# Reordering the first batch's chain of a two-layer mixture-of-experts kernel, with TensorE kept at work before it

## The chip, the cores and the metric

The kernel runs on one core of a Trainium2 chip. The metric is device microseconds for the whole program, the median of three runs.

## The reference

Eight sequences of 1024 tokens with 256 channels, in fp32, go through a "macaron" block: a feed-forward layer, an attention layer, and the same feed-forward layer again with the same weights.

```
x = x + 0.5 * ffn(layernorm(x))
x = x + attention(layernorm(x))       # 16 heads, relu(q), relu(k), linear attention
x = x + 0.5 * ffn(layernorm(x))
ffn(x):
  scores = softmax(x @ gate_w.T);  s = scores + gate_b      # 16 experts in 4 groups
  keep the 2 best groups (sum of their 2 best s), of those the 2 best experts
  y = sum over the 2 experts: scores[e] * ((silu(x@We1[e]+be1[e]) * (x@We3[e]+be3[e])) @ We2[e] + be2[e])
  z = (silu(x@ws1+bs1) * (x@ws3+bs3)) @ ws2 + bs2           # shared expert, 256 inner channels
  return y + z
```

## The kernel before, in words

Names in the text: PE is TensorE, DVE VectorE, ACT ScalarE, POOL GpSimd, SP SyncE (it only issues DMAs). A batch is one of the eight sequences; it has NT = 8 tiles of 128 tokens, and a half is four of them. `r` counts batches over both layers (0 to 15), `L` is the layer, `b` the batch in it.

The program is written by hand engine by engine. Every engine has its own list of instructions, and semaphores (`wait_ge`, `then_inc`) tie them together. One feed-forward layer has two stages: `route(L)` and `experts(L)`.

`route` normalises each batch (DVE takes statistics, POOL raises them to the power -0.5 as `rstd`, DVE makes `nmr`, ACT writes the normalised rows), PE transposes it in four groups `transpose(r, n)` of four 128x128 tiles into the bank `xT_ps`, and ACT copies each group to the transposed activations (`copy_xT`). `gate(r)` on PE makes the scores, DVE copies them (L1188), PE turns them (`turn_scores`), and DVE's generator `choices` picks the experts in some 30 small operations, with one `Exp` on ACT in between. It ends in `sel`; PE's `rank(r)` counts places from it; DVE's `slots(r)` makes the row numbers; ACT's `meta` writes three extra columns; and POOL's `scatter` sends the batch's rows to their expert's region in DRAM, in 16 indirect DMAs, two halves of 8. With `let_through` POOL stops after four sends of each half, and before a batch, until PE has come to a certain part.

Beside all this runs the shared expert, cut in six parts a batch: `up` parts (PE L540, eight instructions of 512 columns each; ACT's silu L896; DVE's gated product L1311) and `down` parts (PE L556, DVE adds to x, L1321). The table `FIRST` says which parts stand in which batch's turn. For later batches DVE takes the choices in small steps between the parts. For batch 0 it does all choices and only then the first two gated products, and PE, which may run only one `up` part ahead of them, does the transposes of batch 1 in one go and waits.

A buffer of normalised rows serves every third batch (`XS` = 3): `normalise(r)` on ACT first waits until the scatter of batch r - 3 has landed. The choices for batch r include the statistics of batch r + 2.

Set-up: POOL writes the constants (identity, ones, and so on) and signals `setup_done`. ACT's queue loads batch 0 in two halves and then the small weights. SP's queue loads `half_bs2` and all biases; with the first half of x landed it issues batch 1, then waits for the biases' split in three bf16 parts by DVE (`bias_split`), stores them, issues batch 2, waits for the store, loads `bias_rows`, and issues the other batches, the experts' weights and the padding. DVE splits the biases first, then does the two halves' statistics of batch 0 (`half_stats`), the first `nmr`, the carry, the second `nmr`, and the statistics of batch 1. The split's scratch memory is in `m.xn`, which is also batch 0's transposed activations, so ACT's first copy waits until the parts are stored.

Of the kernel before, what the change touches and what calls it, by code (L numbers as in the profile page):

```python
# [20 lines left out]
P = 128  # L21
# [285 lines left out]
def program(nc, m, d, sem):  # L307
# [52 lines left out]
    bias_f, bias_r = m.xn[:, 0, 0:nb], m.xn[:, 1, 0:nb]  # L360
    bias_p = m.xn[:, 2, :].bitcast(BF16)[:, 0:3 * nb].rearrange("p (k n) -> p k n", k=3)
# [13 lines left out]
    def piece(n):  # L375
        b, h = divmod(n, PIECES)
        return x_tiles(b, h * NT // PIECES, NT // PIECES)

# [12 lines left out]
    with nc.Block() as block:  # L391
        @block.sync
        def _(sp):
# [54 lines left out]
            sp.wait_ge(s.setup_done, 1)  # L448
# [41 lines left out]
        def _(pe):  # L490
            def transpose(r, n):
                g, c = divmod(n, KC)
                pe.wait_ge(s.xn_half, 2 * r + g + 1)
                wait(pe, s.xT_copied, 4 * r + n)
                if n == 0:
                    wait(pe, s.rank_read, r - 1)
                    if early(r):
                        pe.wait_ge(s.a_xT_copied, 4 * (2 * (r - BATCHES) + 2))
                    if r == BATCHES + EARLY:
                        pe.wait_ge(s.a_xT_copied, 4 * BATCHES)  # L500
                for j in range(4):
                    last = nc.tensor.transpose(xT_ps[:, j * P:(j + 1) * P],
                                               m.xs[buffer_of(r)][:, 4 * g + j, c * P:(c + 1) * P], m.ident[:])
                last.then_inc(s.xT_ready, 1)
# [97 lines left out]
            def route(L):  # L602
                for b in range(LEAD[L], BATCHES):
# [20 lines left out]
                    if b == LEAD[L]:  # L624
                        if L:
                            shared(L, n, turn_and_first_half)
                            shared(L, n + 1, second_half)
                        else:
                            gate(r)
                            shared(L, n, turn)  # L630
                            shared(L, n + 1)
                            for j in range(4):
                                transpose(r + 1, j)
                        rank(r)
                        for j in range(n + 2, end):
                            shared(L, j)
                        continue
# [155 lines left out]
            for n in range(4):  # L793
                transpose(0, n)
# [64 lines left out]
        def _(act):  # L859
# [15 lines left out]
            def copy_xT(r, n):  # L875
# [4 lines left out]
                elif r == 0:  # L880
                    act.wait_ge(s.bias_bounced, 16)
# [6 lines left out]
                nc.scalar.copy(m.xnTs[xnT_of(r)][:, c, g * HALF:(g + 1) * HALF], xT_ps[:]).then_inc(s.xT_copied, 1)  # L888
# [21 lines left out]
            def route(L):  # L910
                for b in range(LEAD[L], BATCHES):
                    r = L * BATCHES + b
                    more = b + 1 < BATCHES
                    n, end = FIRST[L][b - LEAD[L]:b - LEAD[L] + 2]
                    if more:
                        normalise(r + 1)
                    if b == LEAD[L]:
                        exponentials(r)
                        if L:
                            copy_xT(r + 1, 0)  # L920
                        shared(L, n)
                        if L:
                            copy_xT(r + 1, 1)
                            copy_xT(r + 1, 2)
                        shared(L, n + 1)
                        for j in range(3 if L else 0, 4):
                            copy_xT(r + 1, j)
# [180 lines left out]
        def _(dve):  # L1108
# [81 lines left out]
            def route_work(r):  # L1190
# [6 lines left out]
                if ahead:  # L1197
                    yield from stats_work(r + 2)
                yield from choices(r)
# [137 lines left out]
            def route(L):  # L1337
                for b in range(LEAD[L], BATCHES):
# [3 lines left out]
                    if b == LEAD[L]:  # L1342
# [3 lines left out]
                        shared(L, n + 1, iter(()), 0)  # L1346
                        for _ in slots(r):
# [121 lines left out]
            dve.wait_ge(s.bias_loaded, 16)  # L1469
            nc.vector.tensor_copy(bias_p[:, 0], bias_f).then_inc(s.bias_split, 1)  # L1470
            dve.wait_ge(s.bias_split, 1)
            ch.then(TT(bias_r, bias_f, bias_p[:, 0], ALU.subtract))
            nc.vector.tensor_copy(bias_p[:, 1], bias_r).then_inc(s.bias_split, 1)
            dve.wait_ge(s.bias_split, 2)
            ch.then(TT(bias_f, bias_r, bias_p[:, 1], ALU.subtract))
            nc.vector.tensor_copy(bias_p[:, 2], bias_f).then_inc(s.bias_split, 1)
            ch.did(nc.vector.memset(m.ones_b[:], 1.0))
            ch.then(nc.vector.memset(m.sel[:], 0.0))
            def half_stats(h, arrived, ready):
                tiles = slice(h * PAIRS, (h + 1) * PAIRS)  # L1480
                dve.wait_ge(arrived, 16)
                stats(0, range(h * PAIRS, (h + 1) * PAIRS))
# [12 lines left out]

            half_stats(0, s.x_first, s.first_stats)
            half_stats(1, s.x_in[0], s.stats_ready)
# [336 lines left out]
```

## Time and profile before

| | us |
|---|---|
| median of three runs | 1282.25 (1281.26 to 1282.93) |
| the profiled execution, its own time | 1280.93 |
| its span, first to last instruction | 1279.2 |
| PE busy | 1148.5 |
| DVE busy | 860.4 |
| ACT busy | 762.1 |
| POOL busy | 696.8 |

Busy times are of the span; several engines work at once. The mean granted clock of TensorE is 0.973 of full speed. The chain of waits is the list of work that ended last, followed back from the end: only time on it can be saved. A timeline lists an engine's instructions with start and duration, and merges equal ones.

### The profile page before, as it was taken

The page shows a single profiled execution, that of the slowest core. Times are in us where ns is not written, and L with a number is a line of the kernel's source. Part 1 is how long each engine was busy: PE and PEld are TensorE (multiplying, and loading weights), DVE is VectorE, ACT ScalarE, POOL GpSimd, SP SyncE. Part 2 cuts the span into 40 slices and gives each one's busy share as a digit, 9 for nine tenths or more (in the row PEclk, how much of TensorE's full clock was granted, in tenths as well). Part 3 has the DMA queues.
Part 4 walks back from the last instruction along what each step waited for, and adds up shares of the span by engine and source line. Part 5 has one row for each costly group of instructions (what it writes and reads, how often), then busy time and mean ns, then how long its engine had stood idle before and what let it go on. Part 6 is the DMA issues. An engine that isn't in the chain of part 4 may idle for free.

```text
span 1279.2 us, 26244 instructions
## 1 busy us (share of the span) xinstructions
PE 1148.5 (90%) x6640; PEld 899.7 (70%) x6640; DVE 860.4 (67%) x2772; ACT 762.1 (60%) x1700; POOL 696.8 (54%) x850
## 2 busy tenths in 40 slices
PE   4897989899999994999998999899799999999981
PEld 2554555699999974777887878555456999999750
DVE  4686777366666645677778776676753766666487
ACT  4344542388888846575665653544313888888488
POOL 3366767388888873010421503256661888887820
PEclk9899989999999997999999999999999999999996
DMA  9822225656655533011311400012277566555398
GB/s 347 281 76 88 96 84 145 190 174 175 171 172 164 160 96 120 32 67 66 104 64 34 129 21 34 34 67 80 88 204 259 167 172 172 170 166 154 100 400 354
DMA packets 93928, 181.53 MB, mean 142 GB/s; under 512 B 17592, under 2 KB 60368, under 8 KB 91990
## 3 DMA queue, kind: packets, MB, share of 16 engines
q1 hardware_dynamic: 66342, 110.44, 28.2%
q0 software_dynamic: 26016, 67.55, 15.2%
q10 hardware_dynamic: 1424, 1.86, 0.5%
q8 instruction: 59, 0.97, 0.3%
q14 instruction: 87, 0.71, 0.2%
HBM read 97.63 MB, written 86.08 MB: 144 GB/s over the span
## 4 chain that ended last, share of the span: by engine, by line
PE 58%; DVE 17%; ACT 10%; POOL 6%; issue 5%; DMA 3%; SPq 1%; DVEq 0%; ACTq 0%; POOLq 0%
PE bank L681 20%; PE bank L691 10%; PE bank L540 7%; POOL expert_rows L1623 5%; PE bank L556 5%; PE bank L672 5%; PE bank L787 3%; ACT rows L979 2%; PE bank L737 2%; ACT w L979 2%; DVE stat L1120 2%; PE bank L713 2%; ACT xn L997 1%; ACT rows L870 1%; PE bank L515 1%
## 5 line engine op out<-in xcount | busy, mean ns | idle before, releaser
L1686 POOL DMA_INDIRECT routed_rows<-xn,rdest x286 | 282.6, 988 | 114.7 <-DVE xn L1414 44.5
L681 PE MATMUL bank<-rows,att 128*128 128x128 f32 x2288 | 302.4, 275 | 0.4 <-ACT att L968 0.4
L681 PEld LDWEIGHTS bank<-rows,att 128*128 128x128 f32 x2288 | 278.3, 192 | 1.1 <-ACT att L968 0.9
L1623 POOL DMA_INDIRECT expert_rows<-rows,slots x160 | 154.8, 967 | 105.7 <-issue 56.1
L968 ACT COPY att<-w 128x512 f32 x286 | 177.1, 619 | 12.2 <-issue 6.4
L691 PE MATMUL bank<-w,rows 128*128 x572 | 170.8, 381 | 1.6 <-DVE rows L1401 1.4
L1401 DVE SCALAR_TENSOR_TENSOR rows<-bank,tile_b,att 128x128 f32<-128x128 f32 x286 | 100.1, 350 | 107.2 <-ACT att L973 96.4
L967 ACT COPY rows<-bank 128x256 f32<-128x256 f32 x286 | 106.4, 372 | 83.3 <-PE bank L672 77.6
L1414 DVE TENSOR_TENSOR xn<-bank,be 128x256 f32<-128x256 f32 x286 | 121.5, 425 | 33.8 <-issue 11.1
L556 PE MATMUL bank<-ws,be 128*128 128x256 f32 x512 | 124.7, 394 | 8.5 <-DVE be L1311 8.4
L556 PEld LDWEIGHTS bank<-ws,be 128*128 128x128 f32 x512 | 98.6, 197 | 39.5 <-DVE be L1311 17.8
L896 ACT ACTIVATE silu<-bank,bs 128x512 f32<-128x512 f32 x64 | 43.9, 686 | 133.7 <-PE bank L540 133.5
L1675 POOL TENSOR_TENSOR xres<-xres,half_bs 128x128 f32<-128x128 f32 x256 | 117.9, 469 | 3.0
L672 PE MATMUL bank<-ident,rows 128*128 128x128 f32 x572 | 109.0, 273 | 3.1 <-DVE xres L1321 2.1
L973 ACT ACTIVATE att<-bank,tile_b 128x128 f32<-128x128 f32 x286 | 103.5, 362 | 3.8 <-PE bank L681 3.8
L672 PEld LDWEIGHTS bank<-ident,rows 128*128 128x128 f32 x572 | 80.0, 141 | 32.0 <-issue 3.5
L691 PEld LDWEIGHTS bank<-w,rows 128*128 128x128 f32 x572 | 87.0, 192 | 2.6 <-issue 2.5
L1311 DVE SCALAR_TENSOR_TENSOR be<-bank,bs,silu 128x512 f32<-128x512 f32 x64 | 47.8, 750 | 59.1 <-PE bank L540 57.6
L1623 POOL DMA_INDIRECT expert_rows<-w,slots x48 | 48.2, 1004 | 60.3 <-PE bank L713 29.8
L979 ACT ACTIVATE rows<-rows,weights 128x256 f32<-128x256 f32 x176 | 73.7, 498 | 10.2 <-DMA rows<-routed_rows 10.2
L540 PE MATMUL bank<-w,ws 128*128 128x512 f32 x160 | 76.1, 607 | 1.2 <-DVE be L1311 1.2
L1611 POOL TENSOR_TENSOR rstd<-ve,minus_half 128x8 f32<-128x8 f32 x8 | 15.0, 1878 | 113.7 <-DVE ve L1128 113.7
(206 smaller groups left out, 2028.9 us busy)
## 6 DMA issues: line engine op xcount, KB each, us to landing
rows<-expert_rows SPq DMA_DIRECT2D x286, 129.5 KB
rows<-routed_rows SPq DMA_DIRECT2D x32, 512.0 KB, 4.0
w<-routed_rows SPq DMA_DIRECT2D x10, 1024.0 KB, 9.8
w<-in_w SPq DMA_DIRECT2D x2, 4096.0 KB, 18.1
out<-xres SPq DMA_DIRECT2D x16, 512.0 KB, 9.1
xres<-in_x SPq DMA_DIRECT2D x7, 1024.0 KB, 7.2
rows<-routed_rows SPq DMA_DIRECT2D x6, 1024.0 KB, 7.3
expert_rows<-pad SPq DMA_DIRECT2D x47, 129.5 KB, 5.9
```

The source lines that it names most:

```text
L540: last = nc.tensor.matmul(bank[:], ws[:, c, mi * P:(mi + 1) * P], xnT[:, c, g * HALF:(g + 1) * HALF], start=c == 0, stop=c == KC - 1)
L556: last = nc.tensor.matmul(y_ps[j][:, t % 2 * C:(t % 2 + 1) * C], m.gT[:, g, mi, t * P:(t + 1) * P], m.ws2[:, mi, :], start=mi == 0, stop=m ...
L672: last = nc.tensor.transpose(rT_ps[a % 2][:, c * P:(c + 1) * P], m.rin[:, a % SLOTS, c * P:(c + 1) * P], m.ident[:])
L681: last = nc.tensor.matmul(rh_ps[t % RB][:, n * P:(n + 1) * P], m.rw13[:, t % RB, c * C + n * INTER:c * C + (n + 1) * INTER], m.rT[:, t % R ...
L691: nc.tensor.matmul(ry_ps[y % RB][:, 0:C], m.rgT[:, y % RB, :], m.w2[:, bass.ds(e, C)], start=True, stop=True).then_inc(s.ry_ready, 1)
L967: nc.scalar.copy(m.rT[:, a % RB, :], rT_ps[a % 2][:, 0:C]).then_inc(s.rT_copied, 1)
L968: nc.scalar.copy(m.rw13[:, a % RB, :].rearrange("p (c n) -> p c n", c=KC), w13[:, :, bass.ds(expert_at(i + 2), C)]).then_inc(s.rw13_copied, 1)
L979: last = nc.scalar.activation(y[:, k, j * C:(j + 1) * C], y[:, k, j * C:(j + 1) * C], ACT.Copy, scale=m.weights[:, b, k, i:i + 1])
L1414: TT(m.ry[:, n, :], ry_ps[y % RB][:, 0:C], m.be2[:, bass.ds(e, C)], ALU.add).then_inc(s.ry_scaled, 1)
L1623: nc.gpsimd.indirect_dma_start(out=d.xg, out_offset=bass.IndirectOffsetOnAxis(ap=m.slots[:, slots_of(r), k, i:i + 1], axis=0), in_=m.xs[bu ...
L1675: last = nc.gpsimd.tensor_tensor(x, x, m.half_bs2[:, c:c + P], ALU.add)
L1686: nc.gpsimd.indirect_dma_start(out=d.yt, out_offset=bass.IndirectOffsetOnAxis(ap=m.rdest[:, n:n + 1], axis=0), in_=m.ry[:, n, :], in_offse ...
```

## The change

Four things change, all in the first layer's first batch.

1. The biases' scratch moves to `m.att`, and ACT's first copy no longer waits for the store. DVE splits the biases after batch 0's statistics. SP issues batch 1 at the set-up's end, batch 2 when the first half of x has landed, and the small `bias_rows` load after the experts' weights.
2. In batch 0 the transposes go in turn to two banks (`xT_of`); DVE copies groups 0 and 1, ACT groups 2 and 3. ACT normalises the second half before any copy. DVE makes the first `nmr` before it aggregates the second half.
3. In batch 0's turn PE does batch 1's transposes inside parts 2 and 3 and the rank behind part 3. DVE does the choices in steps, six before each of the first two gated products, and a part of batch 2's statistics ahead of the first step. ACT normalises half of batch 1, then does the exponentials, the first silu, the other half.
4. `keep_busy` puts products of constants on PE, with results nobody reads: 20 before the first transposes, 4 after groups 0 and 1, 4 after groups 2 and 3.

```diff
-    bias_f, bias_r = m.xn[:, 0, 0:nb], m.xn[:, 1, 0:nb]
+    scratch = m.att[:, NT * ROW:NT * ROW + 4 * nb]
+    bias_f, bias_r = scratch[:, 0:nb], scratch[:, nb:2 * nb]
...
+    def xT_of(r, n):
+        return y_ps[0] if r == 0 and n % 2 else xT_ps
...
+            sp.wait_ge(s.setup_done, 1)
+            load_x(1)
             sp.wait_ge(s.x_first, 16)
-            load_x(1)
+            load_x(2)
             sp.wait_ge(s.bias_split, 3)
             sp.dma_start(d.bias_parts.rearrange("k (p f) -> p k f", p=P), bias_p).then_inc(s.bias_bounced, 16)
-            load_x(2)
-            sp.wait_ge(s.bias_bounced, 16)
-            sp.wait_ge(s.rows_zeroed, 1)
-            sp.dma_start(m.bias_rows[0:3, :], d.bias_parts[:, BPROJ:BPROJ + C]).then_inc(s.bias_placed, 16)
...
-                wait(pe, s.xT_copied, 4 * r + n)
+                wait(pe, s.xT_copied, 4 * r + n if r else n // 2 * 2)
...
                             shared(L, n + 1)
-                            for j in range(4):
-                                transpose(r + 1, j)
+                            shared(L, n + 2, first_half)
+                            shared(L, n + 3, second_half)
                         rank(r)
-                        for j in range(n + 2, end):
+                        for j in range(n + (2 if L else 4), end):
                             shared(L, j)
...
             pe.wait_ge(s.setup_done, 1)
-            for n in range(4):
-                transpose(0, n)
+            def keep_busy(count):
+                for _ in range(count):
+                    nc.tensor.matmul(h3_ps[1][:, 0:P], m.ones_f[:], m.ident[:], start=True, stop=True)
+            keep_busy(20)
+            transpose(0, 0)
+            transpose(0, 1)
+            keep_busy(4)
+            transpose(0, 2)
+            transpose(0, 3)
+            keep_busy(4)
...
-                elif r == 0:
-                    act.wait_ge(s.bias_bounced, 16)
...
+                    if r == 0:
+                        normalise(1, range(PAIRS))
+                        exponentials(0)
+                        shared(0, n)
+                        normalise(1, range(PAIRS, NT))
+                        shared(0, n + 1)
+                        copy_xT(1, 0)
+                        shared(0, n + 2)
+                        for j in range(1, 4):
+                            copy_xT(1, j)
+                        meta(0)
+                        for j in range(n + 3, end):
+                            shared(0, j)
+                        continue
...
-            copy_xT(0, 0)
             normalise(0, range(PAIRS, NT))
-            for n in range(1, 4):
+            for n in range(2, 4):
                 copy_xT(0, n)
...
+                chosen, ahead_stats = choices(r), stats_work(r + 2) if ahead else iter(())
+                if r == 0:
+                    next(ahead_stats)
+                    next(ahead_stats)
+                    next(chosen)
+                    yield
+                    next(ahead_stats)
+                    for _ in range(5):
+                        next(chosen)
+                        yield
...
-                    if b == LEAD[L]:
+                    if r == 0:
+                        shared(0, n, work, 6)
+                        shared(0, n + 1, work, 6)
+                        for _ in work:
+                            pass
+                    elif b == LEAD[L]:
...
+            dve.wait_ge(s.x_first, 16)
+            stats(0, range(PAIRS))
+            half_aggregate(0, s.first_stats)
+            dve.wait_ge(s.x_in[0], 16)
+            stats(0, range(PAIRS, NT))
             half_negate_mean(0, s.first_rstd, s.first_nmr)
+            half_aggregate(1, s.stats_ready)
+            split_bias()
             dve.wait_ge(s.setup_done, 1)
             ch.then(nc.vector.tensor_copy(m.carry[:], m.region0[:]))
             half_negate_mean(1, s.rstd_ready, s.nmr_ready)
+            for n in range(2):
+                dve.wait_ge(s.xT_ready, n + 1)
+                nc.vector.tensor_copy(m.xnTs[0][:, n, 0:HALF], xT_of(0, n)[:]).then_inc(s.xT_copied, 1)
             route_stats(1)
```

## Rows read from the trace of the kernel before

**Rows 1.** The page, part 4: the chain's share of the span by engine.
```profile
PE 58%; DVE 17%; ACT 10%; POOL 6%; issue 5%; DMA 3%; SPq 1%; DVEq 0%; ACTq 0%; POOLq 0%
```

**Rows 2.** Chain of waits, 70 to 330 us: start, duration, what.
```profile
77.72 0.95 POOL expert_rows L1623
...
98.39 2.45 DMA expert_rows<-rows,slots
```

**Rows 3.** POOL's timeline, 40 to 250 us: start, duration, instruction, idle and releaser.
```profile
43.53 1.21 POOL L1623 DMA_INDIRECT expert_rows<-rows,slots  x1 [11.95 <-issue]
...
58.85 1.67 POOL L1605 TENSOR_TENSOR rstd<-ve,minus_half 128x8 f32<-128x8 f32 x1 [5.26 <-DVE ve L1128]
...
125.74 0.95 POOL L1623 DMA_INDIRECT expert_rows<-rows,slots  x1 [4.39 <-DVE slots L1172]
...
175.47 0.96 POOL L1623 DMA_INDIRECT expert_rows<-att,slots  x1 [5.79 <-DVE slots L1172]
```

**Rows 4.** Chain of waits, 40 to 60 us.
```profile
40.47 6.28 PE bank L540 x8
...
50.21 3.43 PE bank L540 x8
53.64 1.00 PE bank L515 x16
```

**Rows 5.** Timeline of all engines, 0 to 75 us.
```profile
6.82 0.33 SPq L397 DMA_DIRECT2D xres<-in_x  x1
...
8.63 1.41 DVE L1120 BATCH_NORM_STATS2 stat<-xres 128x6 f32<-128x256 f32 x4
...
10.74 1.04 POOL L1736 TENSOR_TENSOR rstd<-ve,minus_half 128x4 f32<-128x4 f32 x1 [6.20 <-DVE ve L1487]
...
12.49 0.15 DVE L1492 SCALAR_TENSOR_TENSOR nmr<-mv,rstd 128x4 f32<-128x4 f32 x1
```

**Rows 6.** Line 1031, batch 0's two loads: from issue to landing.
```profile
DMA to landing us min/median/max: 6.0/6.7/7.5
```

**Rows 7.** Windows, PE: window, length, busy (count), granted clock, DMA share, GB/s.
```profile
39.00:40.00 1.00, 0.58 (x8) 0.50 1.07 459
...
46.00:47.00 1.00, 1.00 (x4) 1.00 0.90 307
```

**Rows 8.** DVE's timeline, 20 to 60 us.
```profile
24.98 0.42 DVE L1188 COPY tile_b<-bank 128x256 f32<-128x256 f32 x1 [4.41 <-PE bank L515]
...
28.92 0.29 DVE L1206 TENSOR_REDUCE mx<-bank 128x8 f32<-128x128 f32 x1
...
35.92 0.29 DVE L1154 TENSOR_TENSOR chosen<-rev,rr 128x128 f32<-128x128 f32 x1
...
39.58 1.41 DVE L1311 SCALAR_TENSOR_TENSOR be<-bank,bs,silu 128x512 f32<-128x512 f32 x2
...
48.52 0.69 DVE L1321 SCALAR_TENSOR_TENSOR xres<-bank,xres 128x512 f32<-128x512 f32 x1 [0.92 <-PE bank L556]
```

**Rows 9.** PE's timeline, 60 to 260 us.
```profile
62.64 0.60 PE L502 MATMUL bank<-ident,att 128*128 128x128 f32 x4
...
75.53 0.44 PE L523 MATMUL bank<-ident,tile_b 128*128 128x128 f32 x2 [1.52 <-DVE tile_b L1188]
...
117.48 0.30 PE L577 MATMUL bank<-sel,before 128*128 128x144 bf16 x1 [3.59 <-DVE sel L1250]
...
118.19 1.94 PE L515 MATMUL bank<-xnT,gate_w 128*32 128x256 f32 x16
...
221.22 1.05 PE L588 MATMUL bank<-ident,tabf 128*128 128x128 f32 x8
```

**Rows 10.** Timelines of ACT and DVE, 50 to 130 us.
```profile
72.51 4.04 ACT L870 ACTIVATE rows<-xres,nmr,rstd 128x256 f32<-128x256 f32 x8 [1.65 <-DMA expert_rows<-rows,slots]
...
81.18 0.31 ACT L901 ACTIVATE ex<-sh 128x128 f32<-128x128 f32 x1 [3.33 <-DVE sh L1207]
...
96.88 0.17 DVE L1172 CAST slots<-slot_f 128x16 uint32<-128x16 f32 x1
```

More of the change, by code:

```diff
@@ L447, in _ @@
                          .to_broadcast([P, E * C // 2])).then_inc(s.be2_in, 16)
-            sp.wait_ge(s.setup_done, 1)
+            sp.wait_ge(s.bias_bounced, 16)
+            sp.wait_ge(s.rows_zeroed, 1)
+            sp.dma_start(m.bias_rows[0:3, :], d.bias_parts[:, BPROJ:BPROJ + C]).then_inc(s.bias_placed, 16)
             for i in range(SPARE_TILES):
@@ L501, in transpose @@
                 for j in range(4):
-                    last = nc.tensor.transpose(xT_ps[:, j * P:(j + 1) * P],
+                    last = nc.tensor.transpose(xT_of(r, n)[:, j * P:(j + 1) * P],
                                                m.xs[buffer_of(r)][:, 4 * g + j, c * P:(c + 1) * P], m.ident[:])
@@ L887, in copy_xT @@
                     act.wait_ge(s.ay_ready, BATCHES * PAIRS)
-                nc.scalar.copy(m.xnTs[xnT_of(r)][:, c, g * HALF:(g + 1) * HALF], xT_ps[:]).then_inc(s.xT_copied, 1)
+                nc.scalar.copy(m.xnTs[xnT_of(r)][:, c, g * HALF:(g + 1) * HALF], xT_of(r, n)[:]).then_inc(s.xT_copied, 1)
             def shared(L, n):
@@ L918, in route @@
                         exponentials(r)
-                        if L:
-                            copy_xT(r + 1, 0)
+                        copy_xT(r + 1, 0)
                         shared(L, n)
-                        if L:
-                            copy_xT(r + 1, 1)
-                            copy_xT(r + 1, 2)
+                        copy_xT(r + 1, 1)
+                        copy_xT(r + 1, 2)
                         shared(L, n + 1)
-                        for j in range(3 if L else 0, 4):
-                            copy_xT(r + 1, j)
+                        copy_xT(r + 1, 3)
                         meta(r)
@@ L1196, in route_work @@
                 yield from placing
-                if ahead:
-                    yield from stats_work(r + 2)
-                yield from choices(r)
+                chosen, ahead_stats = choices(r), stats_work(r + 2) if ahead else iter(())
[8 more added lines that the diff above has]
+                        yield
+                yield from ahead_stats
+                yield from chosen
                 if ahead:
@@ L1468, in _, with half_aggregate @@
             nc.vector.memset(m.bias_rows[:, :].bitcast(U32), 0).then_inc(s.rows_zeroed, 1)
[L1469 to L1476, printed above, removed]
             ch.did(nc.vector.memset(m.ones_b[:], 1.0))
             ch.then(nc.vector.memset(m.sel[:], 0.0))
-            def half_stats(h, arrived, ready):
+            def half_aggregate(h, ready):
                 tiles = slice(h * PAIRS, (h + 1) * PAIRS)
-                dve.wait_ge(arrived, 16)
-                stats(0, range(h * PAIRS, (h + 1) * PAIRS))
                 ch.settle()
@@ L1494, in half_negate_mean, with split_bias @@
                 dve.wait_ge(ready, 1)
-            half_stats(0, s.x_first, s.first_stats)
-            half_stats(1, s.x_in[0], s.stats_ready)
+            def split_bias():
+                dve.wait_ge(s.bias_loaded, 16)
+                nc.vector.tensor_copy(bias_p[:, 0], bias_f).then_inc(s.bias_split, 1)
+                dve.wait_ge(s.bias_split, 1)
+                ch.then(TT(bias_r, bias_f, bias_p[:, 0], ALU.subtract))
+                nc.vector.tensor_copy(bias_p[:, 1], bias_r).then_inc(s.bias_split, 1)
+                dve.wait_ge(s.bias_split, 2)
+                ch.then(TT(bias_f, bias_r, bias_p[:, 1], ALU.subtract))
+                nc.vector.tensor_copy(bias_p[:, 2], bias_f).then_inc(s.bias_split, 1)
+            dve.wait_ge(s.x_first, 16)
[3 more added lines that the diff above has]
+            stats(0, range(PAIRS, NT))
             half_negate_mean(0, s.first_rstd, s.first_nmr)
+            half_aggregate(1, s.stats_ready)
+            split_bias()
             dve.wait_ge(s.setup_done, 1)
```

3 lines of the change are left out of this document (2 added, 1 removed).

## The prediction

> **What bounds the kernel now.** I read the page's shares first, then the chain of waits, then the timelines of each engine over the first 100 us. By the page PE leads the chain for 58% [rows 1]: a saving beside PE's path is lost unless it moves PE, or whatever paces PE. The chain [rows 2] tells which: up to about 74 us it runs through the set-up, DVE's choices for batch 0 and PE; from 77.72 us through POOL's scatters of routed rows. Those pace the rest of the first routing. Scatter(1)'s last send, 98.39, has landed at 100.84, then ACT normalises batch 4 into the same buffer, then come batch 3's choices and scatter(3) at 125.74, scatter(5) at 175.47, and from there sends without a gap to the last of this routing [rows 3]. Each is released by the one before, so whatever moves 77.72 moves the experts' start and, behind it, the end. Sends are 1.265 us apart and not shortened by the change.
>
> So two numbers decide: when gate(1), batch 1's first product on PE, starts (53.64 us now, [rows 4]), since part 9, whose first half releases scatter(1), follows it after 24.1 us (77.72 - 53.64) of PE work at full rate; and whether POOL is free by then.
>
> **Front: to batch 0's scores.** Now SP sees the first half of x at 6.82, but DVE splits the biases until 8.5 and starts statistics at 8.63; its nmr comes at 12.49 [rows 5]. After the change statistics start at about 6.9. From their start to POOL's power took 10.74 - 8.63 = 2.11, so POOL works from 9.0 to 10.05. DVE now does the second half's statistics (1.40) before nmr, and these need the second half of x. The two halves, issued at 0.8 and 1.25, took 6.0 to 7.5 us to land [rows 6]: 6.8 and about 8.7. The load of batch 1 (1 MB) is issued at set-up's end, 4.6 instead of 6.82, so its data meet this half. Bounds: no delay (statistics 9.0 to 10.4), or the 1.9 us between the landings doubled, 10.6 (to 12.0). I take 9.5, nearer the undisturbed landing: nmr from 10.9 to 11.05, 1.4 us earlier than now. The layer's weights follow x on ACT's queue; 1 MB at the 459 GB/s of [rows 7] makes them 2.3 later at most. No group of waits names them now, and gate(0) is covered by DVE (below), so I count nothing.
>
> The second half, alone among large loads, landed 1.9 us behind the first [rows 6], 512 KB in that time. The Trainium skill (DMA: Bandwidth & Descriptors, Queues, rings and completion order) says that a DMA engine takes turns between the queues that hold work for it, packet by packet. By that rule, which speaks against moving batch 1's load forward, the sum would be 1.1 us worse than with my 9.5; without it 0.5 us better.
>
> Then DVE: aggregate and ve to 11.7, POOL's power 11.8 to 12.8, meanwhile the five split operations (bounded by SP's 6.82 and the statistics' 8.63 in [rows 5], two memsets included; I take 1.1) and the carry to 12.95, second nmr 13.1. ACT normalises 11.1 to 13.2 and 13.25 to 15.3 (2.07 each). Transposes 0 and 1 go to two banks without waiting for a copy. DVE copies them: no row has a DVE copy of 128x512. Bounds are ACT's 0.58 and twice the 0.42 of DVE's 128x256 copy; I take 0.69, the time of DVE's 128x512 add out of the same memory [rows 8]. So 13.95 to 15.35. Transposes 2 and 3 follow ACT's second half at 15.4, gate(0) comes at about 17.3 instead of 22.90. But that is not what counts: DVE must finish batch 1's statistics before it copies the scores: 3.59 from the first to after ve (the same work stands between the copy's end at 25.33 and 28.92, [rows 8]), 1.67 for POOL's power [rows 3], and 0.5 for two handovers and nmr. 15.35 + 5.75 = 21.1 against 24.98 now. **Gain 3.9 us.** PE waits for this inside its first part.
>
> **Batch 0's choices.** Now, from the copy of the scores to gate(1), 53.64 - 24.98 = 28.66 us. DVE does all choices, then the first two gated products at 39.58; PE's third part waits for them, and runs at half clock: granted clock 0.50 from 39 on, 1.00 only from 46, after a stretch (34 to 38.7) of four short groups of transposes between copies; eight products take 6.28 us where eight take 3.43 later [rows 4, 7]. After: DVE's work until the second gated product has ended is copy 0.35, statistics of batch 2 3.59 (25.33 to 28.92), choices up to the first rr 7.0 (28.92 to 35.92), two gated products of 0.70 (1.41 for both, [rows 8]): 12.35, at 33.45. The steps are cut so that six come before each of the two. Exp is no wait of its own: ACT normalises only four tiles of batch 1 (2.07) before it, and its silu with the table load (1.3 + 0.7) ends two us before the first gated product. The other PE operations up to here are covered: 1.72 to the turn, 5.2 behind it, 4.33 for part 2 with two transposes, with some 2 us of idle in all. Then PE at full rate: part 3 with two groups of transposes 3.45 + 0.88, rank 0.5, part 4 3.45 (each from [rows 4, 9]): gate(1) is 12.35 + 0.05 + 4.33 + 0.55 + 3.45 = 20.75 after the copy of the scores. **Gain 28.66 - 20.75 = 7.9 us.** From 35.92 to the first gated product at 39.58 were 3.66, with sel, the weights and nmr: sel is done before 33.45 + 3.66 = 37.1, rank comes at 37.85: no wait.
>
> Together gate(1) at 21.1 + 20.75 = 41.85, **11.8 us earlier**.
>
> **Products of constants.** No row has this one; the nearest is L588, 128x128 with ident, eight instructions in 1.05 us, and four products of 128 columns are eight instructions [rows 9]: 0.22 us a product at full rate, 0.44 at half. Twenty from 4.6: 4.4 to 8.8 us, over at 9.0 to 13.4; first transposes come at 13.2. Cost 0 to 0.2, hidden by the front's DVE and ACT. The fours cost 0.9 (1.8 cold), after transposes 1 and 3: the first lies beside ACT's second half, the second beside ACT's two copies; cold, gate(0) is delayed by about 1.0, within DVE's cover (PE idle 1.4 before the turn). If clock is not raised by them, gate(0), 1.0 at full rate, costs 1.97 and the first half part 3.4: 22.7, the logits 0.3 late: cost 0 to 0.5. I take 0. Their value is mostly insurance: the order already removes the sparse stretch. PE is idle some 1.5 us at three places; behind 1.52 idle the rate stayed full, behind 3.59 not (L515's group took 1.94, against 1.00 in [rows 4]) [rows 9].
>
> **SP and POOL.** x(2) goes to 6.9, the bias parts and x(3) onward to 13, at most 1.4 earlier than now; the placing of the biases moves behind the expert loads, needed only in the attention. SP's new early wait for the set-up holds back only loads that now go at 6.82 or later; the pads still follow everything. POOL: slots(0) 1.55 after rank, 40.0; first send 1.1 later at 41.1. Now from 43.53 sixteen sends of 1.265 with rstd in between (1.67 and 0.3) take 22.2, without the wait of 5.26 before 58.85 (for batch 3's statistics, which then are there at 46): POOL free at 63.3. Scatter(1) is wanted at 77.72 - 11.8 = 65.9: 2.6 us of cover. The place of `bias_f` in other memory takes a wait off ACT's first copy; its price lies between 0 and 1.3 (the copy came 12.49 + 3.5), and the front above doesn't use it.
>
> What is late next: normalise(3) needs scatter(0) landed, 2.8 after its last send at 62.3: 65.1, against 72.51 - 11.8 = 60.7 [rows 10]. It ends with its table load at 70.5; exp(2) could start at 81.18 - 11.8 = 69.4. DVE's choices 1.1 late; slots(2) end at 97.05 and the send that needs them is at 99.66 (98.39 + 1.27) [rows 2, 10], so 2.6 hides 1.1.
>
> **Sum.** 3.9 + 7.9 = 11.8 us off the profiled execution's 1280.93 (span 1279.2, 1.7 around it): 1269.1. The median of the runs, 1282.25, lies 1.3 higher; from it 1270.4, which I predict for the changed kernel's median.
>
> **Rivals.**
> - *The scatter loop keeps part* (0.13): normalise(3) comes only 7.4 us earlier. If its lateness of 4.4 is passed on by ACT's order (copies and silu behind exp) past the 2.6 of cover, the gain is 7.4 to 10: 1274.9. For: ACT waits for landed sends in each batch from here. Against: the slack at slots(2), and normalise(4), which depends on scatter(1), not on scatter(0).
> - *The front gives nothing* (0.09): the load of x late, or DVE copying and splitting ahead of batch 1's statistics eats the gain; only 7.9 stays: 1274.4. Against: two copies are 1.4 us and the split 1.1, both counted.
> - *Better than I count* (0.08): load undisturbed (0.5), DVE's copies at 0.58 (0.2), and a later latency of PE or DVE shortened where the loop's two gaps on POOL (4.4 at 125.74, 5.8 at 175.47) shrink with the new phase, by 1.5 of their 10.2: 1268.2.
> - *Slower: the clock* (0.04): PE's many short idles keep it at half from gate(0) on. Content from there to gate(1) is 1.0 + 0.22 + 4 x 3.45 + 3.45 + 1.76 + 0.5 = 20.8 at full rate, 41.5 at half: gate(1) at 17.3 + 41.5 = 58.8, 5.2 late: 1287.5. It turns slower when more than 13.8 of the 20.8 run at half (11.8 gained and 2 of idle). For: a sparse stretch did this at 39. Against: busy share after 17.3 is about 0.9.
> - *It does nothing* (0.03): scatter pace set elsewhere, another wait at 77.72: 1282.
>
> **Chances.** Forecast 0.63 (its own range 1268.5 to 1272.5, by the bounds of the load, -0.5 to +1.1, and of the copies, -0.2 to +0.3). Range 1266.5 to 1277: it holds the best counting and the two partial cases, and leaves out the clock and no effect; 8 in 10 or a bit more, as the DMA and copy bounds make it. What this kernel's measurement can tell from no change is 0.2%, 2.6 us: faster 0.92, within 0.04, slower 0.04.
>
> **What would show it.** nmr at 10.9; scores copied at 21.1; rate of L540 at 0.43 a product from gate(0); second gated product at 33.4; gate(1) at 41.9; first send 41.1; scatter(1) at 65.9; scatter(3) at 113.9, scatter(5) at 163.7; experts the same in length. Wrong if gate(1) moves and 77.72 moves less, or if the later scatters don't follow.

## The result

| | before | after |
|---|---|---|
| median of the runs, us | 1282.05 (4 runs, 1281.26 to 1282.93) | 1268.8 (4 runs, 1268.31 to 1271.33) |
| profiled execution, its own time and span | 1280.93, 1279.2 | 1268.79, 1267.1 |

The ratio is 0.9895, with a 95% interval from 0.9882 to 0.9907: 13.3 us faster by the medians, 12.1 by the profiled executions. Predicted were 1270.4 and a gain of 11.8. The single marks stand as follows.

| mark, start in us | before | forecast | after | moved by |
|---|---|---|---|---|
| first nmr | 12.49 | 10.9 | 10.10 | -2.4 |
| batch 0's scores copied | 24.98 | 21.1 | 20.03 | -5.0 |
| gate(1) | 53.57 | 41.9 | 40.23 | -13.3 |
| first send | 43.53 | 41.1 | 39.52 | -4.0 |
| scatter(1) | 77.72 | 65.9 | 64.55 | -13.2 |
| scatter(3) | 125.74 | 113.9 | 113.90 | -11.8 |
| scatter(5) | 175.47 | 163.7 | 162.38 | -13.1 |
| last send of the first routing | 235.04 | | 221.94 | -13.1 |
| first send of the experts' results | 254.10 | | 241.51 | -12.6 |

The page of the changed kernel has the same shape as before [rows 1].

```profile
span 1267.1 us, 26351 instructions
...
PE 56%; DVE 18%; ACT 9%; POOL 6%; issue 5%; DMA 4%; SPq 1%; DVEq 0%; ACTq 0%; POOLq 0%
```

The timeline of all engines, 0 to 75 us, shows the new front; it answers to [rows 5] and [rows 8]. Read DVE from its statistics at 6.85 to the second gated product at 30.97.

```profile
4.62 2.48 SPq L401 DMA_DIRECT2D xres<-in_x  x2
4.64 6.08 PE L799 MATMUL bank<-ident,ones_f 128*128 128x128 f32 x40 [4.64 <-POOLq L1775]
...
6.85 1.40 DVE L1141 BATCH_NORM_STATS2 stat<-xres 128x6 f32<-128x256 f32 x4 [5.57 <-DMA xres<-in_x]
...
8.78 1.40 DVE L1141 BATCH_NORM_STATS2 stat<-xres 128x6 f32<-128x256 f32 x4
...
10.10 0.14 DVE L1519 SCALAR_TENSOR_TENSOR nmr<-mv,rstd 128x4 f32<-128x4 f32 x1
...
12.40 1.09 PE L506 MATMUL bank<-ident,rows 128*128 128x128 f32 x8 [1.68 <-ACT rows L1059]
13.16 1.29 DVE L1546 COPY xn<-bank 128x512 f32<-128x512 f32 x2 [0.93 <-PE bank L506]
...
14.37 2.70 DVE L1141 BATCH_NORM_STATS2 stat<-xres 128x6 f32<-128x256 f32 x8
...
16.73 1.07 PE L519 MATMUL bank<-xn,gate_w 128*32 128x256 f32 x16 [0.18 <-DMA bs<-in_bs]
...
18.16 1.64 POOL L1650 TENSOR_TENSOR rstd<-ve,minus_half 128x8 f32<-128x8 f32 x1 [6.18 <-DVE ve L1149]
...
20.03 0.42 DVE L1209 COPY tile_b<-bank 128x256 f32<-128x256 f32 x1
...
30.97 0.75 DVE L1341 SCALAR_TENSOR_TENSOR be<-bank,bs,silu 128x512 f32<-128x512 f32 x1
...
31.77 1.13 PE L560 MATMUL bank<-ws,be 128*128 128x256 f32 x4 [0.47 <-DVE be L1341]
```

The second half's statistics at 8.78 carry no idle time: batch 1's early load, issued at 4.62, did not hold them up. Gate(0) at 16.73 runs at full rate (1.07 for sixteen), 3.3 us before DVE can copy its scores.

From 38 to 260 us the chain of waits is what paces the rest; it answers to [rows 2] and [rows 4]. The half clock of 39 to 46 us is gone, but two later places keep theirs (L519 is the gate, L560 the down part).

```profile
60.40 2.63 DMA expert_rows<-rows,slots
63.12 4.04 ACT rows L883 x8
...
85.19 2.79 DMA expert_rows<-rows,slots
...
105.50 1.87 PE bank L519 x16
107.37 3.21 PE bank L560 x8
...
154.67 1.86 PE bank L519 x16
156.54 2.52 PE bank L560 x8
```

The same chain before, 118 to 174 us, has 2.30 us for the down part (L556 there) behind batch 3's gate and 3.73 for that behind batch 5's:

```profile
120.13 2.30 PE bank L556 x8
...
168.43 3.73 PE bank L556 x8
```

So scatter(3) lost 0.9 us to the clock and scatter(5) got 1.2 back. That is most of the difference between the moves: -13.2 at scatter(1), -11.8 at scatter(3), -13.1 at scatter(5). That scatter(3) stands on its forecast to the hundredth is luck: it was 1.3 us ahead at scatter(1) and lost them on the way. POOL's timeline, 30 to 250 us, shows its idle time before scatter(1), 3.19 us where 2.6 were forecast [rows 3].

```profile
39.52 1.21 POOL L1668 DMA_INDIRECT expert_rows<-rows,slots  x1 [8.59 <-issue]
...
49.60 1.68 POOL L1650 TENSOR_TENSOR rstd<-ve,minus_half 128x8 f32<-128x8 f32 x1
...
64.55 0.96 POOL L1668 DMA_INDIRECT expert_rows<-rows,slots  x1 [3.19 <-PE bank L560]
...
113.90 0.96 POOL L1668 DMA_INDIRECT expert_rows<-rows,slots  x1 [5.84 <-DVE slots L1193]
...
162.38 0.96 POOL L1668 DMA_INDIRECT expert_rows<-att,slots  x1 [4.72 <-DVE slots L1193]
```

### The profile page after: what moved, and what is told of

It is laid out like the page before. It is cut to its first block, busy times and chain, and to the rows that moved or that the text cites. A ratio compares the mean times of both kernels' runs of the same rounds, so it can differ in the third digit from the quotient of the medians.

```text
span 1267.1 us, 26351 instructions
## 1 busy us (share of the span) xinstructions
PE 1149.6 (91%) x6696; PEld 904.2 (71%) x6696; DVE 862.2 (68%) x2774; ACT 761.6 (60%) x1698; POOL 696.6 (55%) x850
## 4 chain that ended last, share of the span: by engine, by line
PE 56%; DVE 18%; ACT 9%; POOL 6%; issue 5%; DMA 4%; SPq 1%; DVEq 0%; ACTq 0%; POOLq 0%
PE bank L685 20%; PE bank L695 10%; PE bank L544 5%; PE bank L560 5%; PE bank L676 5%; POOL expert_rows L1668 5%; PE bank L791 3%; PE bank L741 2%; ACT rows L1001 2%; DVE stat L1141 2%; PE bank L717 2%; ACT rows L883 1%; ACT xn L1019 1%; DMA expert_rows<-rows,slots 1%; DMA w<-routed_rows 1%
## 5 line engine op out<-in xcount | busy, mean ns | idle before, releaser
L1450 DVE TENSOR_TENSOR xn<-bank,be 128x256 f32<-128x256 f32 x286 | 121.5, 425 | 35.0 <-issue 13.1
L560 PE MATMUL bank<-ws,be 128*128 128x256 f32 x512 | 124.9, 394 | 8.5 <-DVE be L1341 8.5
L560 PEld LDWEIGHTS bank<-ws,be 128*128 128x128 f32 x512 | 98.4, 197 | 40.0 <-DVE be L1341 18.6
## 6 DMA issues: line engine op xcount, KB each, us to landing
w<-routed_rows SPq DMA_DIRECT2D x10, 1024.0 KB, 12.1
```

The costliest lines, as they stand in the source:

```text
L560: last = nc.tensor.matmul(y_ps[j][:, t % 2 * C:(t % 2 + 1) * C], m.gT[:, g, mi, t * P:(t + 1) * P], m.ws2[:, mi, :], start=mi == 0, stop=m ...
L1450: TT(m.ry[:, n, :], ry_ps[y % RB][:, 0:C], m.be2[:, bass.ds(e, C)], ALU.add).then_inc(s.ry_scaled, 1)
```

## The experiments

Whole times scatter by several us from run to run on the chips used here (the kernel before: 1276.6 to 1288.3), while gate(1) and the last send of the first routing agree within 0.3 us in the two profiles of the changed kernel (e0 below). So each experiment is read by its ratio and, for its place, by these two marks. They have noise of their own: e4 has the front of the kernel before, unedited, and yet its first nmr is at 13.07 instead of 12.49. In between, single transfers vary more. Batch 0's last send takes 2.63 us to land in the changed kernel's profile and 5.44 in e8's, ahead of anything e8 adds. Each experiment has one profile, so differences under about 0.6 us at a mark are not told from nothing.

| run | ratio to before (95%) | gate(1) | last send |
|---|---|---|---|
| before | 1 | 53.57 | 235.04 |
| changed | 0.9895 (0.9882 to 0.9907) | 40.23 | 221.94 |
| e0 changed, again | 0.9901 (0.9884 to 0.9917) | 40.27 | 222.22 |
| e1 no products | 0.9919 (0.9897 to 0.9940) | 42.33 | 223.21 |
| e2 products alone | 1.0015 (1.0001 to 1.0029) | 51.73 | 233.38 |
| e3 old order of the choices | 0.9956 (0.9929 to 0.9984) | 48.25 | 230.41 |
| e4 new order alone | 0.9945 (0.9926 to 0.9965) | 47.94 | 229.57 |
| e11 front alone | 0.9962 (0.9949 to 0.9976) | 48.38 | 230.11 |
| e5 batch 1's load later | 0.9897 (0.9869 to 0.9925) | 40.37 | 222.44 |
| e6 split first | 0.9919 (0.9892 to 0.9946) | 41.41 | 223.38 |
| e7 one bank | 0.9912 (0.9884 to 0.9941) | 41.24 | 223.61 |
| e10 twenty products only | 0.9906 (0.9888 to 0.9924) | 40.46 | 221.10 |
| e8 products before two ranks | 0.9878 (0.9851 to 0.9904) | 40.15 | 221.45 |
| e9 products at four idles | 0.9874 (0.9855 to 0.9893) | 40.38 | 218.86 |

**The parts, taken out or put in alone.** e1 takes the products out of the changed kernel:

```diff
-            keep_busy(20)
             transpose(0, 0)
             transpose(0, 1)
-            keep_busy(4)
             transpose(0, 2)
             transpose(0, 3)
-            keep_busy(4)
```

> The changed kernel without the 28 products of constants. My theory (order and front carry the gain, the products almost nothing): gate(0) starts at 16.7 as now but at half clock, so the gate and the first half part take 2.0 + 3.4 us, the logits come at 22.5 instead of 20.95 and DVE, ready at 21.7, waits 0.8 us; part 3 starts some 0.6 later. 0.6 to 1.4 us slower than the changed kernel, 1269.6. Rival (the clock carries the gain): the granted clock stays at half through batch 0's parts and 5 us or more are lost, 1274 or above.

Gate(1) came 2.1 us later: more than forecast, far less than the rival's 5. Its PE timeline, 10 to 40 us:

```profile
12.64 1.94 PE L506 MATMUL bank<-ident,rows 128*128 128x128 f32 x8 [12.64 <-ACT rows L1056]
15.46 1.94 PE L506 MATMUL bank<-ident,rows 128*128 128x128 f32 x8 [0.88 <-DVE xn L1543]
18.17 1.93 PE L519 MATMUL bank<-xn,gate_w 128*32 128x256 f32 x16 [0.77 <-ACT xn L896]
20.03 3.47 PE L544 MATMUL bank<-xn,ws 128*128 128x512 f32 x4
23.34 0.38 PE L527 MATMUL bank<-ident,tile_b 128*128 128x128 f32 x2
```

I had counted the gate and the half part, and left out the transposes: each group of eight takes 1.94 instead of about 1.07, so gate(0) is at 18.17 and the turn (L527) at 23.34 instead of 20.51. The loss comes in two pieces. DVE's copies of the transposes end 0.9 us later, and with them its statistics of batch 1 and the copy of the scores (20.89 instead of 20.03). Then DVE waits 1.13 us for the turn. At the last send 1.3 of the 2.1 us are left, because rank, gate and down part of batch 3 took 0.7 us less in e1: there the gate ran at full rate (1.00). e2 puts the same products into the kernel before:

```diff
-            for n in range(4):
-                transpose(0, n)
+            keep_busy(20)
+            transpose(0, 0)
+            transpose(0, 1)
+            keep_busy(4)
+            transpose(0, 2)
+            transpose(0, 3)
+            keep_busy(4)
```

> The kernel before with only the 28 products of constants, put at the same places of PE's order. My theory: transposes and gate of batch 0 run at the full rate, the copy of the scores moves from 24.98 to about 22.5, the chain behind it keeps its length and its half clock at 39 to 46; 2.0 to 2.8 us faster than before, 1279.7. Rival (the clock carries the gain): PE stays at full clock from there on and 5 us or more are gained, 1277 or below. Second rival: nothing, because the front hangs on ACT and DVE.

Gate(1) moved by 1.84 and the last send by 1.66, a little under the forecast; the total didn't get faster. Between the last send and the end its profile is 3.7 us longer than that of before, and e0 (below) shows that this stretch varies by such an amount in one and the same kernel. But twelve runs against 22 put the ratio at 1.0001 to 1.0029, which leaves out the forecast gain of 2 us. The 1.7 us of the last send did not reach the end, and why stays open. Its windows of PE (length, busy and count, granted clock, DMA share, GB/s) show that they did not hold the clock among the old order's single transposes:

```profile
14.00:16.00 2.00, 0.66 (x4) 1.00 0.75 230
16.00:18.00 2.00, 1.74 (x10) 0.68 0.97 385
18.00:20.00 2.00, 1.73 (x8) 0.50 0.98 406
20.00:22.00 2.00, 1.45 (x12) 0.97 1.04 430
```

e3 is the changed kernel with batch 0's turn as before, e4 the kernel before with only that turn new, both on all three engines. Of e3's edit, PE's part is shown; ACT's and DVE's orders go back in the same way:

```diff
...
                             shared(L, n + 1)
-                            shared(L, n + 2, first_half)
-                            shared(L, n + 3, second_half)
+                            for j in range(4):
+                                transpose(r + 1, j)
                         rank(r)
-                        for j in range(n + (2 if L else 4), end):
+                        for j in range(n + 2, end):
...
```

> The changed kernel with batch 0's turn as before (all choices first, batch 1's transposes in one go, rank before part 2), front and products kept. My theory: the copy of the scores stays at 20.0, the chain from it to gate(1) takes 28.7 instead of 20.2 us again, with the sparse stretch and half clock in it: 8.4 us slower than the changed kernel, 1277.2. Rival (the scatter loop sets the pace, and part of the order's gain is lost in it anyway): 5 to 7 us slower, 1275.

> The kernel before with only batch 0's turn in the new order; old front, no products. My theory: the copy of the scores at 24.98 as before, gate(1) 20.2 to 21 us after it instead of 28.7: 7.7 to 8.4 us faster than before, 1274. Rival (without products PE is cold for the parts and the order gains little): 3 to 5 us faster, 1278.

e3: gate(1) 8.0 later, close to the forecast of 8.4. The last send is 8.5 later and the total some 0.6% slower: little is lost in the scatter loop. e4: 5.6 earlier, where 7.7 to 8.4 were forecast and 3 to 5 by the rival; gate(1) follows the copy of the scores (25.56) after 22.4 instead of 20.2 us. PE was at half rate at the start of batch 0, and in the new order that costs: the turn comes 3.35 us behind the copy, 0.48 in the changed kernel. Another 0.6 is the late front named above, so the order itself gave 6.2 (28.6 - 22.4). e11 is the third part alone, the changed kernel with the edits of e1 and e3 together:

> The kernel before with only the new front (split later, loads earlier, two banks with DVE's two copies): old order of batch 0's turn, no products. If parts add up: products alone gave gate(1) 1.84 earlier and the order alone 5.6 of the 13.34, so the front has up to 5.9; with the products it gave 5.3. Without them I expect gate(1) 3.2 to 4.2 us earlier than before (49.4 to 50.4). Rival (the front hangs on DVE alone): 5.3 earlier also without products.

It gave 5.2, the rival's value, not mine: with the old order the products add only 0.1 to the front at gate(1) (48.38 against 48.25). They do bring the third part 0.7 us forward (35.35 in e3, 36.08 in e11), but this part then takes 5.9 us in e3 and 5.3 in e11, because e3's half clock set in earlier. PE's windows, e3 first, then e11:

```profile
30.00:32.00 2.00, 1.14 (x5) 0.50 1.10 475
```

```profile
30.00:32.00 2.00, 1.08 (x8) 1.00 0.99 426
```

In e11 the granted clock stands at 0.50 only from 34 us. That both effects nearly cancel is an outcome of these two profiles, not a rule. At gate(1) the parts alone give 1.8 + 5.6 + 5.2 = 12.6 of 13.3, so they nearly add, though which of them is paid for the clock depends on the company it is in. In the totals they add less well: by the ratios e2 has +0.15%, e4 -0.55% and e11 -0.38%, together -0.8% where the whole change has -1.05%.

**Inside the front.** e5 delays batch 1's load, e6 moves the split ahead, e7 goes back to one bank:

```diff
             sp.wait_ge(s.setup_done, 1)
+            sp.wait_ge(s.x_first, 16)
             load_x(1)
-            sp.wait_ge(s.x_first, 16)
             load_x(2)
```

```diff
+            split_bias()
             dve.wait_ge(s.x_first, 16)
...
             half_aggregate(1, s.stats_ready)
-            split_bias()
```

```diff
-                wait(pe, s.xT_copied, 4 * r + n if r else n // 2 * 2)
+                wait(pe, s.xT_copied, 4 * r + n)
...
-        return y_ps[0] if r == 0 and n % 2 else xT_ps
+        return xT_ps
```

> The changed kernel with batch 1's load issued only when the first half of x has landed (6.85 instead of 4.62 us). In the changed kernel's trace the second half's statistics start at 8.78 with no wait, so the early load did not delay them: no difference (-0.3 to +0.3). Rival (large loads share the queues' turns): the second half and the weights, whose last one gate(0) waited 0.18 for, land sooner, and 0.3 to 0.6 us are gained. Second rival: batch 1's statistics at 14.37 then wait for its landing, up to 2 us lost.

> The changed kernel with the biases' split ahead of batch 0's statistics, as before. The first nmr moves from 10.10 to about 11.5 (statistics start at 8.3 instead of 6.85), and everything up to gate(1) with it, since the later place of the split (10.77 to 11.85) lay beside POOL's power: 1.4 us slower. Rival: the split's 1.1 us were on DVE's path either way, and DVE had 0.93 us of idle before its copies: 0 to 0.5 us slower.

> The changed kernel with batch 0's transposes in one bank again, each waiting for the copy before it; DVE still copies groups 0 and 1, ACT 2 and 3. The second transposes start when DVE's first copy ends (13.82) instead of at once, so DVE's second copy and batch 1's statistics behind it come 0.7 to 0.9 later, and everything to gate(1) with them: gate(1) at 41.0, 0.8 slower. Rival: DVE's time is set by POOL's power for batch 1, and ACT's two copies in turn delay gate(0) only: no difference.

e5: no difference at gate(1) (0.14 later, ratio 0.9897), first theory right. The loads themselves do differ. Of the layer's weights, which follow x on ACT's queue, the slowest load landed 10.9 us after its issue in the changed kernel and 6.1 in e5 (7.9 in the kernel before). This is the line of these loads (L1056), first in the changed kernel, then in e5:

```profile
DMA to landing us min/median/max: 5.6/8.3/10.9
```

```profile
DMA to landing us min/median/max: 4.9/5.2/6.1
```

So batch 1's early load holds the weights up by about 4.8 us. Gate(0) waits for them 0.18 us in the changed kernel, 0.88 in e3 and 1.33 in e10, and it costs nothing only because DVE copies the scores later still. e6: 1.2 later at gate(1), as at the first nmr (11.27): the theory was off by 0.2, the rival wrong. e7: 1.0 later at gate(1) and at the copy of the scores (21.03), of which 0.1 was there at the first nmr, so the second bank is worth about 0.9. The wait for POOL's power is 1.88 us in both profiles. It moves with DVE's statistics ahead of it and doesn't hide the delay.

e10 leaves only the first twenty products.

```diff
             transpose(0, 1)
-            keep_busy(4)
             transpose(0, 2)
             transpose(0, 3)
-            keep_busy(4)
```

> The changed kernel with the first 20 products and without the two groups of four. If the first twenty raise the clock and the transposes after them hold it, gate(0) comes 0.0 to 0.3 earlier and nothing else moves: gate(1) at 40.0 to 40.2. Rival (the fours are needed to hold the clock over the idle beside ACT and DVE): the gate or a part falls to half rate, and gate(1) comes 1 to 2 us later.

Gate(1) 40.46 against 40.23, of which 0.21 was there at the first nmr, and the gate at full rate (1.07 in the PE timeline of 4 to 24 us, below). The fours are not needed here. Gate(0) came no earlier, as I had expected, but 0.5 us later (17.21), because it waited 1.33 for the last weight.

```profile
4.64 7.11 PE L799 MATMUL bank<-ident,ones_f 128*128 128x128 f32 x40 [4.64 <-POOLq L1773]
12.62 1.09 PE L506 MATMUL bank<-ident,rows 128*128 128x128 f32 x8 [0.86 <-ACT rows L1057]
14.82 1.06 PE L506 MATMUL bank<-ident,rows 128*128 128x128 f32 x8 [1.11 <-DVE xn L1544]
17.21 1.07 PE L519 MATMUL bank<-xn,gate_w 128*32 128x256 f32 x16 [1.33 <-DMA bs<-in_bs]
```

**Where the clock still falls.** e8 and e9 put products into the idle time of PE that the chain shows before ranks 3 and 5 (e9 also before layer 2's rank 13, and 68 before the attention's first transposes):

```diff
             def rank(r):
                 ranks = ranks_of(r)
-                pe.wait_ge(s.sel_ready, r + 1)
                 if not early(r):
                     pe.wait_ge(s.xT_copied, 4 * (r + 1 if r % BATCHES == BATCHES - 1 else r + 2))
+                if r in (3, 5):
+                    for _ in range(14):
+                        nc.tensor.matmul(xT_ps[:, 0:P], m.ones_f[:], m.ident[:], start=True, stop=True)
+                pe.wait_ge(s.sel_ready, r + 1)
```

```diff
             pe.wait_ge(s.bias_placed, 16)
+            pe.wait_ge(s.rT_copied, TILES)
+            for _ in range(68):
+                nc.tensor.matmul(xT_ps[:, 0:P], m.ones_f[:], m.ident[:], start=True, stop=True)
             for n in range(4):
                 a_transpose(0, n)
```

> The changed kernel with 14 more products of constants (3.0 us at full rate) before the ranks of batches 3 and 5, where PE is idle for 3.6 us waiting for sel and then runs the rank, the gate and part of a down part at half clock (gate 1.87 instead of 1.00, eight products of L560 3.21 and 2.52 instead of 1.73). My theory: the chain of waits runs through just these, so 2.3 us at batch 3 and 1.7 at batch 5 come back and pass through the scatter loop to the end: 2.5 to 4 us faster than the changed kernel, 1265.5. Rival: POOL's unbroken sends or the experts' loads set the end of the routing, and less than 1 us is gained.

> The changed kernel with products of constants at every long idle of PE: 15 before the ranks of batches 3 and 5 and of batch 5 of layer 2, and 68 (14.6 us at full rate) in the 16.7 us in which PE waits for the attention's first transposes. In e8 the two of layer 1 moved scatter(5) by 2.9 us but the last send by 0.5 only, and the total by about 2. My theory: the attention's start, two groups of four transposes at 0.97 and twelve products at 3.11 us on the chain, gives 2 to 2.5 us more, layer 2's rank 1 to 2: 4 to 6 us faster than the changed kernel, 1264. Rival: what comes behind (ACT's weighing, POOL's sends, DVE's choices) takes it back, as in e8, and it is level with e8, 1267.

e8's products worked locally. In its PE timeline, 96 to 116 us, gate and down part are at full rate (3.37 us of products instead of idle):

```profile
102.15 3.37 PE L582 MATMUL bank<-ident,ones_f 128*128 128x128 f32 x28
...
105.78 1.07 PE L519 MATMUL bank<-xnT,gate_w 128*32 128x256 f32 x16
106.78 1.99 PE L560 MATMUL bank<-ws,be 128*128 128x256 f32 x8
```

Scatter(3) came 1.8 and scatter(5) 2.9 us earlier, but the last send only 0.5: POOL's timeline, 155 to 225 us, has a new wait for PE ahead of batch 6's sends (182.06, below). The rival's direction was right, with PE's part as the release that holds POOL. This profile is not a clean comparison, though. POOL has such waits ahead of batch 2 (89.21, 2.94 us) and batch 4 (136.34, 2.54) too, and the first comes before any added product: batch 0's last send landed late, ACT normalised batch 3 at 65.83 instead of 63.12, and batch 2's turn moved with it. This is the mechanism of the prediction's first rival. The chain of e8, 58 to 68 us, shows the landing, and then POOL's two lines follow.

```profile
60.30 5.44 DMA expert_rows<-rows,slots
```

```profile
159.46 0.95 POOL L1671 DMA_INDIRECT expert_rows<-att,slots  x1 [1.52 <-issue]
182.06 0.96 POOL L1671 DMA_INDIRECT expert_rows<-rows,slots  x1 [2.65 <-PE bank L544]
```

In e9 the last send is 3.1 earlier, but at the attention's start only 0.3 of it is left (the second group of transposes at 485.62 against 485.91), and a rank of layer 2 starts at 765.31, at 765.37 in the changed kernel. What lies between varies by more than that in e0, so the cause stays open. The chain of e9, 455 to 500 us, has the same loads, ACT weighing and POOL power as that of the changed kernel, which no product shortens:

```profile
462.83 3.92 DMA rows<-routed_rows
466.77 1.72 ACT rows L1007 x4
...
478.79 1.68 POOL rstd L1662
481.47 2.34 ACT xn L1025 x5
485.62 1.72 PE bank L710 x8
```

The first group of eight transposes ran at full rate (1.09, in the changed kernel 1.94), but it isn't on the chain. The second took 1.72 here, 1.94 in the changed kernel, and the twelve products behind it 3.62, where the changed kernel has 3.11: the clock was not held over the waits for ACT, and the expected 2 to 2.5 us were not had. In total e9 ran at 1267.14 beside e0's 1270.96 on the same chip (1264.86 to 1267.59 against 1267.53 to 1272.58), e8 at 1267.12 beside e5's 1270.88 on another. So e9 is level with e8, as its rival said; I had forecast 1264. These two have the lowest ratios measured here, but their intervals overlap that of the changed kernel; a gain of 0.2 to 0.3% over it is likely and not proved.

**What the runs scatter by.** e0 is the changed kernel, unedited.

> The changed kernel itself once more, beside the kernel before on this chip, as the reference for what runs with it: ratio 0.9895 as measured, 0.987 to 0.992.

Gate(1) (40.27) and the last send (222.22 against 221.94) agree with the first profile; between them normalise(3) is 1.4 us later (64.53). Then PE's timeline, 219 to 245 us, differs: loads of expert rows come later and the clock falls again, and the span ends at 1270.8 instead of 1267.1 us.

```profile
229.88 0.41 PE L676 MATMUL bank<-ident,rows 128*128 128x128 f32 x2 [1.29 <-DMA rows<-expert_rows]
...
231.09 0.44 PE L676 MATMUL bank<-ident,rows 128*128 128x128 f32 x2 [0.80 <-DMA rows<-expert_rows]
...
234.07 1.92 PE L685 MATMUL bank<-rows,att 128*128 128x128 f32 x8
```

The first profile has 1.06 in place of 1.92. Of the 3.4 us that e0 loses behind the last send, 1.2 lie ahead of the first send of the experts' results (242.96 against 241.51); where the others arise was not traced.

## Why the prediction was right

The sum had two terms, a front of 3.9 and a turn of 7.9 us, passed on whole by the scatters. They measured 5.0 (at the copy of the scores) and 8.4 (from there to gate(1)).

- *The front* was undersized by 1.1. Of this 0.8 is the load: I took 9.5 us for the second half's statistics, because batch 1's load meets it; they started at 8.78 without a wait. The slower of batch 0's two loads landed 7.2 us after its issue, 7.5 before and 7.3 in e5. By the rule of the Trainium skill (DMA: Bandwidth & Descriptors, Queues, rings and completion order) that queues take turns, the second half should have landed later; it did not. The weights behind it on the same queue did: 10.9 us for the slowest, 6.1 in e5 where batch 1's load is issued later, so there the trace agrees with the rule. My bound for them, 2.3 us later at most, was too small (3.0 against before, 4.8 against e5), and only the cover at gate(0) kept it out of the sum. The rest of the 1.1 is DVE's two copies, 1.29 together where 1.4 was taken, and 0.2 between them and the copy of the scores. e7 shows that the second bank is worth about 0.9 of the gain, e6 that the later split is worth 1.2.
- *The turn* was undersized by 0.5: from the copy of the scores to the end of the second gated product 11.7 instead of 12.35. Before, DVE waited about 0.4 us for Exp and one of its operations, `sc`, took 0.47; now batch 2's statistics lie beside Exp, and `sc` takes 0.29. PE's terms (4.33, 0.5, 3.45) hold; e3 gives the turn's 8.0 by itself.
- *The products* are where I was wrong in size: I put them at 0, as insurance. They are worth 2.1 us at gate(1) and 1.3 at the last send in the new order (e1), and 0.1 beside the old order and new front (e11, e3). The failed step is "cost 0 to 0.5" for a clock that they do not raise: it counted the gate and half a part at half rate, and not the sixteen transposes ahead of them, whose copies DVE makes. The forecast total was not touched, since its terms had been counted at full rate; it took for granted the clock that the products bring.
- *POOL and the loop*: POOL free 3.2 us before scatter(1), normalise(3) at 63.12 (65.1 forecast). The chain of the changed kernel does pass through it, so that first rival was near. It took little from scatter(1)'s successors: scatter(3)'s loss of 1.3 is 0.9 of clock and 0.4 that was not traced. How near it was depends on one landing: with 5.44 us for it in e8, POOL stood 2.94 us ahead of batch 2's sends.
- *The end*: 13.1 at the last send became 12.1 in the profiled execution and 13.3 in the medians. e0 shows that the stretches behind vary by more than what lies between, so no cause in the change is needed for it; that there is none isn't shown (e2's gain did not reach the end). The first microseconds of that difference are later loads and a lower clock; why the loads came later wasn't settled. So a total within 1.6 us of the forecast says less than the marks do: two profiles of one kernel end 3.7 us apart.

## What to carry to other kernels

Find the loop that paces the stage (here landed scatters of one batch release the normalising of a later one) and ask only what starts it: 13 us won at the first gate arrived at the last send 180 us later. An engine that waits for another's long chain should get that chain cut into steps between its own small duties; this was the largest single part. Products of constants are worth what is at half rate behind them and on the chain, the smallest work included, so count every matmul and transpose up to the next full-rate stretch.

## What the runs showed of the hardware that I had not expected

- The same first 40 instructions of constants took between 6.08 us (the changed kernel) and 7.21 us (e2) in ten profiles. From 8 to 10 us PE did 20 of them in the changed kernel and 11 in e2, so the full rate came at different times in the two. The granted clock reads 1.00 over the whole stretch of 4 to 12 us in both, and also over 24 to 28 us in the kernel before, where the instructions of L540 start 0.86 us apart (0.43 at full rate). So early in the program the durations tell the rate, and the clock column doesn't.
- Batch 1's 1 MB load, issued at 4.62 instead of 6.95 us (e5), made the slowest load of the weights on the other queue land 10.9 us after its issue instead of 6.1, while the 512 KB of x ahead of the weights kept its 7.2.
- After an idle of about 3.6 us before a rank, the down part behind the gate took 2.30 to 3.73 us in different executions or batches, 1.73 at full rate; a routing loop passes such a difference on to its next scatter.
- The landing of one and the same indirect send (batch 0's last) took from 2.63 us in the changed kernel to 5.44 in e8.
